# VectorE takes over the wait for landed scatters, and the third block of a tile is gathered behind the scatters, in a mixture-of-experts tail on one core

## The reference, cut to what matters

```
x = x + conv_attention(layernorm_channels(x))        # 2 x 1024 tokens, 256 channels
t = to_tokens(x)                                     # 2048 tokens x 256
xt = layernorm(t)
gate = softmax(xt @ Wg)                              # 8 experts
topv, topi = top_k(gate, 2); topv /= sum(topv) + 1e-6
out = 0
for e in range(8):
    h = gelu(xt @ W1[e] + b1[e])                     # 256 -> 1024
    out += (h @ W2[e] + b2[e]) * scores[:, e]        # 1024 -> 256; scores are 0 but for the two chosen
t = t + out
```

## Time and profile before

| | us |
|---|---|
| median of 3 runs | 409.2 (409.16 to 413.54) |
| the profiled execution: its own time | 412.29 |
| its span | 410.5 |
| PE busy | 366.2 (89%) |
| DVE busy | 255.5 (62%) |
| ACT busy | 254.9 (62%) |
| POOL busy | 193.4 (47%) |

### The profile page before, as it was taken

One profiled execution on the slowest core, in us unless ns is written; L12 is line 12 of the kernel. 1 busy time (PEld: TensorE's weight loads), 2 busy tenths in 40 slices (PEclk: granted clock), 3 DMA queues, 4 the chain that ended last, 5 costly groups with the idle time before them and its releaser, 6 DMA issues.

```text
span 410.5 us, 8295 instructions
## 1 busy us (share of the span) xinstructions
PE 366.2 (89%) x2500; PEld 330.8 (81%) x2501; DVE 255.5 (62%) x650; ACT 254.9 (62%) x555; POOL 193.4 (47%) x233
## 2 busy tenths in 40 slices
PE   5989978999999797899998999888999998979950
PEld 4535557887889786899998999888999998969950
DVE  5868477797766996554476448754476845635530
ACT  2587556668657773755677459773677757735520
POOL 5800000002026555336675757675666866856553
PEclk9799989999998967999999999998999999989995
DMA  8710000000011772628316632756316533232342
GB/s 279 250 38 2 0 1 2 0 2 0 2 59 46 311 267 91 240 73 212 65 44 180 140 54 42 257 154 141 65 41 171 125 55 65 28 65 52 53 61 29
DMA packets 22966, 38.62 MB, mean 94 GB/s; under 512 B 2577, under 2 KB 17297, under 8 KB 22801
## 3 DMA queue, kind: packets, MB, share of 16 engines
q1 hardware_dynamic: 14896, 25.41, 17.8%
q0 software_dynamic: 8032, 12.82, 17.6%
HBM read 28.85 MB, written 9.37 MB: 93 GB/s over the span
## 4 chain that ended last, share of the span: by engine, by line
PE 57%; issue 11%; DVE 11%; POOL 10%; ACT 5%; POOLq 2%; DVEq 1%; DMA 1%; ACTq 0%
PE banks L1274 9%; PE banks L1276 9%; PE banks L1275 9%; PE banks L1614 6%; PE banks L1618 6%; PE banks L1616 6%; POOL xg L524 5%; PE banks L1389 3%; POOL out_rows L574 3%; PE banks L1312 3%; ACT prob L678 1%; PE banks L1573 1%; DVE expx L918 1%; DVE y_out L1213 1%; DVEq L341 1%
## 5 line engine op out<-in xcount | busy, mean ns | idle before, releaser
L821 ACT ACTIVATE h_raw<-banks,b1t 128x256 f32<-128x256 f32 (+1 forms) x136 | 68.0, 500 | 79.7 <-PE banks L1276 79.3
L574 POOL DMA_INDIRECT out_rows<-y_out,idx_out x36 | 82.7, 2296 | 39.3 <-DVE y_out L1213 33.5
L1222 DVE TENSOR_TENSOR h_lo<-h_raw,h_hi 128x256 fp32r<-128x256 f32 (+1 forms) x136 | 58.0, 438 | 66.1 <-ACT h_hi L824 60.6
L1614 PE MATMUL banks<-w_hi,h_hi 128*128 128x256 f32 x288 | 84.4, 293 | 11.4 <-DVE h_lo L1222 11.4
L1618 PE MATMUL banks<-w_hi,h_lo 128*128 128x256 f32 x288 | 81.9, 284 | 0.0
L1616 PE MATMUL banks<-w_lo,h_hi 128*128 128x256 f32 x288 | 81.9, 284 | 0.0
L1274 PE MATMUL banks<-x_hi,w_hi 128*128 128x256 f32 (+1 forms) x272 | 79.7, 293 | 0.8 <-DVE x_lo L1251 0.5
L1275 PE MATMUL banks<-x_lo,w_hi 128*128 128x256 f32 (+1 forms) x272 | 79.4, 292 | 0.0
L1276 PE MATMUL banks<-x_hi,w_lo 128*128 128x256 f32 (+1 forms) x272 | 79.3, 291 | 0.0
L524 POOL DMA_INDIRECT xg<-xn_rows,idx_in x57 | 58.2, 1021 | 27.9 <-POOL idx_in L518 16.3
L824 ACT ACTIVATE h_hi<-banks,b1t 128x256 fp32r<-128x256 f32 (+1 forms) x136 | 67.8, 498 | 0.0
(11 more groups left out here) (220 smaller groups left out, 669.9 us busy)
## 6 DMA issues: line engine op xcount, KB each, us to landing
w_raw<-in_w SPq DMA_DIRECT2D x16, 1024.0 KB, 7.9
xn_rows<-xn SPq DMA_DIRECT2D x2, 1056.0 KB, 4.7
x<-in_x_tok SPq DMA_DIRECT2D x4, 512.0 KB, 5.5
out_rows<-x SPq DMA_DIRECT2D x1, 2048.0 KB, 9.3
b2b<-in_b SPq DMA_DIRECT2D x1, 1024.0 KB, 4.7
xg<-xn_rows,idx_in POOLq DMA_INDIRECT x57, 3.3
out_rows<-y_out,idx_out POOLq DMA_INDIRECT x36, 3.9
out_rows<-x POOLq DMA_DIRECT2D x1, 384.0 KB, 3.2
```

What stands on the lines that cost most here:

```text
L574: pool.indirect_dma_start(out_d, bass.IndirectOffsetOnAxis(ap=idx_out[:, i:i + 1], axis=0), y_out[:, i, :], None, compute_op=ALU.add).then ...
L821: act.activation(h_raw[j % RING][:, 0:w], banks[:, j % RING, 0:w], ACT.Gelu, bias=bias)
L1222: dve.tensor_tensor(h_lo[:, j, 0:w], h_raw[j % RING][:, 0:w], h_hi[:, j, 0:w].bitcast(F32), ALU.subtract).then_inc(h_split, 1)
L1614: pe.matmul(out, h_hi[:, j, r], w_hi[e % 2][:, c], start=j == 0 and i < 2, stop=False, skip_group_check=width == WIDE)
```

## The change

The wait for landed scatters moves from POOL to DVE: the semaphore `y_free` is gone, and y_scaled(t) waits for `y_added` itself, at a count that DVE keeps in a register: 16 at first, and at the end of each tile the 16 x width of the tile before is added to it. POOL's gather(n) issues only two of the three DMAs; the third one, `gather_block(t + 2, 2)`, is issued behind the scatters of tile t and ahead of move_scores(t + 1). For tiles 0 and 1 the third one is issued right behind the other two. PE's code is unchanged: turn_x still waits for all three blocks.

```diff
-        y_free = sem("y_free")
 ...
                 pool.sem_inc(gathers_begun, 1)
-                for i in range(WIDE):
-                    done = first_gathered[i] if isinstance(n, int) and n == 0 else x_gathered
-                    pool.indirect_dma_start(xg[:, i, :], None, xs_d,
-                                            bass.IndirectOffsetOnAxis(ap=idx_in[:, i:i + 1], axis=0)
-                                            ).then_inc(done, 16)
+                for i in range(2):
+                    gather_block(n, i)
+
+            def gather_block(n, i):
+                done = first_gathered[i] if isinstance(n, int) and n == 0 else x_gathered
+                pool.indirect_dma_start(xg[:, i, :], None, xs_d,
+                                        bass.IndirectOffsetOnAxis(ap=idx_in[:, i:i + 1], axis=0)
+                                        ).then_inc(done, 16)
 ...
             gather(0)
+            gather_block(0, 2)
 ...
             gather(1)
+            gather_block(1, 2)
 ...
                 pool.wait_ge(idx_out_set, t + 1)
-                pool.sem_inc(y_free, 1)
-
                 pool.wait_ge(y_weighted, t + 2)
                 pool.sem_inc(adds_begun, 1)
                 for i in range(width):
                     pool.indirect_dma_start(out_d, bass.IndirectOffsetOnAxis(ap=idx_out[:, i:i + 1], axis=0),
                                             y_out[:, i, :], None, compute_op=ALU.add).then_inc(y_added, 16)
+                gather_block(t + 2, 2)
                 move_scores(t + 1)
 ...
+            added = dve.alloc_register("added")
+            last_blocks = dve.alloc_register("last_blocks")
+            dve.reg_mov(added, 16)
+            dve.reg_mov(last_blocks, 0)
+
             def y_scaled(t, e):
 
-                dve.wait_ge(y_free, t + 1)
+                dve.wait_ge(y_added, dve.snap(added, min_val=16, max_val=48 * TMAX))
                 dve.wait_ge(scores_moved, t + 1)
 ...
                 ins.then_inc(y_taken, 1)
-
-
+                dve.reg_alu(added, added, last_blocks, ALU.add)
+                dve.reg_mov(last_blocks, 16 * width)
```

## The result

The changed kernel takes 481.3 us (median of 4, 479.4 to 483.4) against 410.4 us of the kernel before on the same chips: the ratio is 1.172, 95% interval [1.162, 1.181]. It is 71 us slower; 471 us was forecast. The profiled execution took 479.7 us with a span of 477.9.

A forecast was written before the change was run, and what follows sets the result against it. It took PE, busy 89% of the span, and its standstills to bound the kernel; 412.3 + 45.1 (loops) + 17.7 (clock) - 0.3 (end) = 474.8 us, less 3.1 for the median: 471 us, range 445 to 488.

The forecast's parts named there:

- VectorE's wait goes: Ahead of y_scaled: all 19.6 us of DVE's wait go, and with them PE's stalls for h_lo, 10.3 us.
- Register arithmetic at 0: In DVE's queue: register arithmetic and the wait on a register cost 0, bounds 0 and 0.3 us a tile.
- Two gathers ahead are worth nothing: In POOL's queue: one gather fewer ahead of the scatters gains nothing, since scatters cannot start before y_scaled.
- The loop from turn to turn: Turn, scatters, third gather, next turn: 14.57 us in unsplit tiles, 17.40 in splitting ones, +45.1 us in all.
- The stretched scatters: POOL's scatters in splitting tiles stay long beside DVE's w_lo and h_lo: 6.46 us in tile 10 against 3.63 unsplit.
- the second rival: Scatters don't stretch in their new positions: 19.1 us off the forecast, near 452 us; chance 10%.
- the rule that I weighed: Trainium skill, SBUF: by it w_lo and h_lo shouldn't stretch a scatter; the forecast went by the trace instead.
- The clock: Lower PE clock behind new stalls: 1.47 us for eight long ones, 0.73 for eight short ones, 17.7 us together.
- The end: Last tile: y_out's wait of 1.58 us goes, a third gather lands last, -0.3 us.
- The rival on the other side: At turn_x: the third block is in time and only DVE's gain is left, 397 us; chance 4%.

The follow-up runs named there:

- e1_three_ahead: The changed kernel with all three gathers issued together again ahead of the scatters, VectorE still waiting for y_added itself: 403.1 us, ratio 0.977 to the kernel before.
- e2_third_late_alone: The changed kernel with VectorE waiting through y_free from GpSimd as before, the third gather still behind the scatters: 482.4 us, ratio 1.169 to the kernel before.
- e4_filled_stalls: The changed kernel with 13 matmuls on constants ahead of turn_x's wait, filling TensorE's stalls: 470.3 us, ratio 1.142 to the kernel before.
- e5_w_lo_filled: The kernel before with the eight w_lo subtractions of each splitting tile replaced by fills with zero: 403.2 us, one run.
- e3_third_own_count: The changed kernel with third gathers on their own semaphore, TensorE's turn waiting for it only ahead of tile 11: 433.2 us, ratio 1.052 to the kernel before.
- e9_after_w_lo_filled: The changed kernel with the eight w_lo subtractions of each splitting tile replaced by fills with zero: 466.9 us, ratio 1.136 to the kernel before.

## Why the prediction came out as it did

**VectorE's wait goes.** Right: its wait and PE's wait for h_lo have no row after, and e1_three_ahead gives the gain by itself. Register arithmetic at 0: e2_third_late_alone, without it, is no faster (482.4 against 481.3).

**Two gathers ahead are worth nothing.** Right: scatters still wait for y_out (2.90 us in tile 15).

**The loop from turn to turn.** Right in mechanism and named the largest term. Its parts in tile 15, forecast and measured: to the first scatter 7.34 and 7.30, scatters 3.63 and 3.53, issue 0.30 and 0.31, landing 3.3 and 3.63, and then 0.29 from the landing to PE's transposes, which I had left out. The last two are 0.6 us short, and with the 0.1 us that the scatters were shorter the unsplit tile is 15.06 against 14.57 us, 0.5 us short. With the clock high (e4_filled_stalls) the eight unsplit tiles take 121.0 us together against 116.6. The whole sum there is 265.9 against the forecast's 259.6, so this term was 6.3 us too small, or 3.7 without the unexplained stall of 2.63 us. Why a gather behind a scatter lands 0.3 us later wasn't tested; the last scatter, which lands 3.9 us after its start, is still under way then, and that is only argued.

**The stretched scatters.** The direction was right against the second rival, the size was not: in tile 6 they took
```profile
272.21 3.13 POOL L576 DMA_INDIRECT out_rows<-y_out,idx_out  x1 [4.05 <-DVE y_out L1221]
275.65 2.09 POOL L576 DMA_INDIRECT out_rows<-y_out,idx_out  x1 [0.30 <-issue]
```
5.53 us where 6.46 was forecast, and in tile 11 4.23 us from 362.25 to 366.48 where 8.56 was. This hid part of what was short elsewhere, and it is luck that the two nearly cancel in the splitting tiles (17.22 to 17.45 us in tiles 6, 7 and 13 of e4_filled_stalls against 17.40). Of the rule that I weighed I had used half: the same section of the Trainium skill (SBUF — State Buffer, Who interferes with whom) says that a DVE instruction with two SBUF inputs contends with a GpSimd instruction that reads SBUF. An indirect DMA takes its row numbers from a tile in SBUF, so with that half the rule and the fills of e5_w_lo_filled agree. Whether that read is what is held up was not isolated.

**The clock.** Forecast 17.7 us, which counts the stall ahead of tile 16's turn too, though the time behind it falls into the end. Measured: at least 11 by the medians; by the profiles 14.6 in the sum, or 17.2 without the unexplained stall, and 1.5 at the end. So its size was about right, in part because two misses offset each other, one long stall fewer and more falls behind short ones. Tile 11, counted among the long stalls, had only 0.48 us of one. Behind each of the other seven (4.25 to 5.05 us) the clock fell, and behind six of the eight short ones (2.90 to 3.14 us), where I had taken half. Stalls of that length go either way: behind tile 15's turn, 2.90 us late, tile 16's stretch has a clock of 0.90; behind tile 14's, 2.98 us late, tile 15's has 1.00.

**The end.** Forecast -0.3 us, measured +2.4: from the last turn to the end of the span 477.9 - 457.47 = 20.4 us against 410.5 - 392.48 = 18.0. This is the one step that came out with the wrong sign. The forecast had no clock in it, though the last turn has a stall ahead of it like the others; in e4_filled_stalls the same stretch is 464.0 - 445.04 = 19.0 us, so 1.5 us is the clock. What is left, +0.9 us where -0.3 was forecast, has two parts, read in e4_filled_stalls. The first scatter comes 451.51 - 445.04 = 6.47 us behind the turn against 400.05 - 392.48 = 7.57 before (POOL's timelines), so 1.1 us went and not 1.6. The third gather starts 1.91 us behind the last scatter, and from its start to the end of the span it is 8.65 us, where from the last scatter's start it was 8.51 before: 2.05 us came and not 1.3.

**Together.** Against 471 us the measured 481.3 is 10 us more. The profiles give 480 against my 475 (+2.7 us at the end, +3.2 in the sum with the clock, less 1.0 at the front), and the rest is that the median of the changed kernel lies 1.6 us above its profiled execution, where that of the kernel before lay 3.1 below at the time.

**The rival on the other side** (the third block is in time) was off by all of its mechanism: no third block was in time for its turn in any of 16 tiles. The nearest was that of tile 11's turn, 0.48 us late; all others were 2.90 us late or more. What I had not thought of is that the loop has a second branch through POOL, which makes the new place of the gather costly even where nobody on PE waits for it.

## What to carry to other kernels

When a transfer is moved behind work that depends on its own consumer, write down the loop that this closes and add it up: the tile can't be shorter than that, and a row with slack today (4.3 us ahead of the turn) shows how little there is to spend. Look for each waiter on the moved transfer, since taking the wait off one engine can leave a nearly equal loop on another. A short stall on TensorE costs more than its length where the clock falls behind it, and a faster tile can run into a weight load that used to come after it.

## What the runs showed of the hardware that was not expected

- Fills of 0.48 us between subtractions of two SBUF tensors leave GpSimd's scatters at a median of 1.6 us and 2.28 at most; beside the same pieces as subtractions they take 4.06 and 6.58 us. Gathers are stretched too: one in tile 7 of e3_third_own_count took 3.25 us where 1.0 is usual, beside subtractions too.
- A gather issued 1.7 us behind the release of a 2 MB load landed 8.8 us after issue instead of 3.3, at a DMA share of 1.01. Starting one of the load's two halves 6 us ahead of the other (213.24 and 219.28) was enough to take that off PE's path.
- TensorE stalls of 2.90 to 3.14 us brought the lower clock behind six of eight and not behind the others, of 2.94 and 2.98 us. In e9_after_w_lo_filled nine of eleven stalls of 2.86 to 3.18 us had it behind them, and those of 3.08 and 2.94 us did not. Stalls of 1.46, 1.88 and 2.29 us left the clock at 1.00.
